# A decoder layer: the GRU's 128-row products as pairs of 64-row products

## What is computed

```python
Pn = rmsnorm(P, input_norm_w)                # P: (4, 64, 256)
k_proj, v_proj = Pn @ Wk.T, Pn @ Wv.T
for _ in range(3):                           # slots: (4, 1024, 256)
    q_proj = rmsnorm(slots, slot_norm_w) @ Wq.T
    scores = einsum('bkd,bmd->bkm', q_proj, k_proj) * SCALE
    attn = softmax(scores, axis=-2)          # over the 1024 slots
    attn = attn / (sum(attn, axis=-1, keepdims=True) + EPS)
    updates = einsum('bkm,bmd->bkd', attn, v_proj)
    slots = gru_cell(updates, slots, ...)    # r, z, n gates
```

## Time and profile before

| | us |
|---|---|
| median of three runs | 556.05 (555.78 to 556.29) |
| the profiled execution | 555.52 |
| its span, first to last instruction | 553.7 |
| PE busy | 504.1 |
| weight loads (PEld) busy | 363.6 |
| VectorE busy | 440.0 |
| ScalarE busy | 340.5 |
| GpSimd busy | 251.7 |
| products of line L1456, 1,128 of them | 149 to 484 of the span |

### The profile page before, as it was taken

How to read it: one execution, slowest core, us unless ns; L and a number is a source line. 1 busy time by engine, 2 the same in 40 slices (tenths; PEclk the granted TensorE clock), 3 DMA queues, 4 the chain that set the end, 5 groups by cost and what they waited for, 6 DMA issues and landing times.

```text
span 553.7 us, 7262 instructions
## 1 busy us (share of the span) xinstructions
PE 504.1 (91%) x2154; PEld 363.6 (66%) x2154; DVE 440.0 (79%) x794; ACT 340.5 (61%) x600; POOL 251.7 (45%) x217
## 2 busy tenths in 40 slices
PE   6999986959779999899999999999997999979992
PEld 2465552725557687488768867885885788767771
DVE  2999999998799487989967985897677567868882
ACT  4557539784697574667466656765663766557452
POOL 0123050400223256556835664575335156737776
PEclk9999999879889999999999999999997999989997
DMA  8950435420021031000000000002111136255742
GB/s 286 336 189 2 124 67 140 125 78 1 0 77 72 6 78 77 0 2 0 2 0 1 0 0 1 1 2 76 40 38 38 39 126 237 87 163 161 235 138 71
DMA packets 30661, 43.13 MB, mean 78 GB/s; under 512 B 7933, under 2 KB 22398, under 8 KB 30336
## 3 DMA queue, kind: packets, MB, share of 16 engines
q1 hardware_dynamic: 27216, 34.25, 20.5%
q0 software_dynamic: 3408, 8.43, 4.2%
HBM read 25.70 MB, written 16.83 MB: 77 GB/s over the span
## 4 chain that ended last, share of the span: by engine, by line
PE 51%; issue 6%; DVE 6%; POOL 4%; ACT 3%; DMA 1%; SPq 0%; POOLq 0%; ACTq 0%; DVEq 0%
PE psum L1456 35%; PE psum L1549 7%; PE psum L1267 3%; PE psum L1398 2%; PE psum L1520 2%; PE psum L1344 1%; POOL gru L1019 1%; DVE gru L1872 1%; POOL out L1057 1%; POOL sorted_rows L1049 1%; DVE slots_full L1874 1%; POOL slots_lo L1034 1%; PE psum L1356 1%; DVE gru L1852 1%; PE psum L1420 1%
## 5 line engine op out<-in xcount | busy, mean ns | idle before, releaser
L1456 PE MATMUL psum<-slots_hi,w_hh 128*128 128x512 f32 x560 | 181.5, 406 | 1.2 <-ACT gru L766 1.2
L1456 PEld LDWEIGHTS psum<-slots_hi,w_hh 128*128 128x128 f32 x560 | 104.5, 191 | 27.9 <-issue 4.2
L1019 POOL TENSOR_TENSOR gru<-slots_full,gru 128x512 f32<-128x512 f32 x43 | 65.9, 1531 | 111.6 <-ACT gru L772 111.6
L1456 PE MATMUL psum<-slots_lo,w_hh 128*128 128x512 f32 x280 | 112.3, 401 | 0.0
L1456 PE MATMUL psum<-at,v_ih_pair 128*128 128x512 f32 x288 | 92.6, 406 | 4.6 <-DVE at L1751 3.1
L772 ACT ACTIVATE gru<-gru,vec 128x512 f32<-128x512 f32 x48 | 34.7, 722 | 59.1 <-DVE gru L1852 59.0
L1456 PEld LDWEIGHTS psum<-at,v_ih_pair 128*128 128x128 f32 x288 | 54.6, 193 | 21.6 <-DVE at L1751 3.4
L1845 DVE SCALAR_TENSOR_TENSOR gru<-psum,vec,gru 128x512 f32<-128x512 f32 x48 | 35.9, 748 | 35.6 <-PE psum L1456 29.8
L1152 PE MATMUL psum<-early_hi,w_in 128*128 128x512 f32 x128 | 57.3, 606 | 5.2 <-DMA early_hi<-in_xT 5.1
L1456 PEld LDWEIGHTS psum<-slots_lo,w_hh 128*128 128x128 f32 x280 | 53.4, 191 | 12.9
L1872 DVE TENSOR_TENSOR gru<-gru 128x512 f32<-128x512 f32 x47 | 43.7, 930 | 7.2 <-POOL gru L1019 3.7
(11 more groups left out here) (249 smaller groups left out, 868.1 us busy)
## 6 DMA issues: line engine op xcount, KB each, us to landing
gathered<-sorted_rows SPq DMA_DIRECT2D x39, 129.0 KB, 2.4
x_scratch<-slots_full SPq DMA_DIRECT2D x8, 512.0 KB, 3.0
x_block<-x_scratch SPq DMA_DIRECT2D x8, 512.0 KB, 4.3
early_hi<-in_xT SPq DMA_DIRECT2D x3, 1024.0 KB, 5.7
v_ih_pair<-value_part SPq DMA_DIRECT2D x32, 96.0 KB, 2.2
x_tm<-in_x SPq DMA_DIRECT2D x4, 512.0 KB, 7.0
slots_full<-expert_plus SPq DMA_DIRECT2D x1, 2048.0 KB, 10.1
sorted_rows<-gru SPq DMA_DIRECT2D x1, 1032.0 KB, 11.4
```

Source lines behind the costliest of these rows:

```text
L1019: pool.tensor_tensor(DF(u), full[:, c, seq(k, h), blk(j)], X(u), ALU.subtract).then_inc(d_pool, 1)
L1456: last = pe.matmul(psum[:, bank, :], w, d, start=start and i == 0, stop=stop and i == len(pairs) - 1, skip_group_check=begun or late)
```

## The change

From unit (1,1) to unit (4,6), 30 units, every product on 128 rows becomes two products on 64 rows each, one with the lower half of the partitions ("low rows") and one with the upper ("high rows"). `both` writes them in turns. The two of a pair go to different banks, as they belong to different sums: the low rows run ahead and the high rows follow. In a unit the low rows do r, hn, xn and z of their own unit; the high rows do xn and z of the unit before and then r and hn. The high rows of a sum begin only when its low rows are done, by the new semaphore `low_rows`, on which PE waits for itself.

Of the four half products in a gate's update, low weight by low attention is left out. The product with the low weight is needed on one half only, and is given to the low or the high rows so that both have the same number: 45 half products a unit. For this the high attention must also be had on the other half, in `at_x`, to which SP copies it by a DMA of 64 rows for each h (`copy_attention`).

`attention` and its spread for h = 0 are made in two halves of 512 tokens, the first between t2 of unit 6 and mix of unit 5, the second after it. The spread for h = 1 goes ahead of candidate of unit 2, `tops` behind candidate of unit 3. Mean squares stay in unit 2, but stand after its first eight or nine pairs, scores stand there in unit 3 and sums in unit 6 (before: in unit 5, after xn). ScalarE's and GpSimd's orders are as before; the counts they wait for are adapted.

```diff
+        def at_made(k, h, j):
+
+            n = 2 * k + h
+            return n + 1 + n // 2 - (1 if k > 0 and h == 0 and j == 0 else 0)
...
+        at_x = parts_of_value[:, 0:T]
...
+                def copy_attention(k, h):
+
+                    n = 2 * k + h
+                    sp.wait_ge(at_hi, at_made(k, h, J - 1))
+                    if n > 2:
+                        sp.wait_ge(at_copied, 16 * (n - 2))
+                    if k > 1:
+                        sp.wait_ge(z_mm, U * (n - 1))
+                    sp.dma_start(at_x[half(1 - h), :].bitcast(F32),
+                                 at[n % 3][half(h), :].bitcast(F32)).then_inc(at_copied, 16)
+
+                copy_attention(1, 0)
                 sp.dma_start(ew_dram, expertT).then_inc(plus_out, 16)
...
+                def both(lows, highs):
+
+                    low = high = None
+                    for i in range(max(len(lows), len(highs))):
+                        if i < len(lows):
+                            bank, w, d, start = lows[i]
+                            low = pe.matmul(psum[:, bank, :], w, d, start=start, stop=False, skip_group_check=True)
+                        if i < len(highs):
+                            bank, w, d, start = highs[i]
+                            high = pe.matmul(psum[:, bank, :], w, d, start=start, stop=True, skip_group_check=True)
+                    return low, high
...
+                def split_unit(k, q, before, between=None, last=False):
...
+                    def hidden(bank, gate, rows):
+                        return [(bank, wh[w][rows, i, cols(gate)], slots[d][rows, i, b, blk(j)],
+                                 rows == lo and (i, w, d) == (0, 0, 0)) for i in range(C) for w, d in PASSES]
+
+                    def update(bank, gate, rows, with_low):
+                        first = [(bank, vp(0, b)[rows, cols(gate)], a[rows, blk(j)], rows == lo and gate == 2)]
+                        high_part = a if rows == half(h) else at_x
+                        return first + [(bank, vp(1, b)[rows, cols(gate)], high_part[rows, blk(j)], False)][0:with_low]
+
+                    r_hid, hn_lo = hidden(r, 0, lo), hidden(hn, 2, lo)
+                    r_hi, hn_hi = hidden(r, 0, hi) + update(r, 0, hi, 0), hidden(hn, 2, hi)
...
+                        pe.wait_ge(t_dve, u - 1)
+                        one, two = r_hid, hn_lo
...
+                    if x_before:
+                        pe.wait_ge(low_rows, 4 * n_split - 5)
+                    low, high = both(one[0:2], x_before)
+                    if x_before:
+                        high.then_inc(xn_mm, 1)
+                        pe.wait_ge(low_rows, 4 * n_split - 4)
+                    low, high = both(one[2:], z_before[0:4])
...
+                    if q % J == 0 and q // J < J + 1:
+                        pe.wait_ge(at_lo, at_made(k, h, j))
...
+                    if not swapped:
+                        low, high = both(update(r, 0, lo, 1), z_before[4:6])
+                        low.then_inc(low_rows, 1)
+                        pe.wait_ge(r_act, u)
+                        low, high = both(two[0:max(nz - 6, 1)], z_before[6:])
+                        two = two[max(nz - 6, 1):]
+                        if z_before:
+                            high.then_inc(z_mm, 1)
+                    if "R" in between:
+                        between["R"]()
...
+                        pe.wait_ge(low_rows, 4 * n_split - 3)
+                        n = len(two)
+                        low, high = both(two, r_hi[0:n])
+                        low.then_inc(low_rows, 1)
+                        highs = r_hi[n:]
...
+                    if last:
+                        low, high = both([], highs)
+                        high.then_inc(r_mm, 1)
+                        pe.wait_ge(low_rows, 4 * n_split - 2)
+                        low, high = both([], hn_hi)
+                        high.then_inc(hn_mm, 1)
+                        pe.wait_ge(t2_dve, u)
+                        for w in range(2):
...
+                        mm.then_inc(z_mm, 1)
+                        return [], []
+                    pe.wait_ge(t2_dve, u)
+                    low, high = both(update(XN_B, 2, lo, 0), highs[0:1])
+                    low.then_inc(low_rows, 1)
+                    highs = highs[1:]
...
+                    pe.wait_ge(z_act, u - 1)
+                    z_lo = hidden(z, 1, lo) + update(z, 1, lo, u % 2)
+                    n = len(highs)
+                    low, high = both(z_lo[0:n], highs)
...
+                        high.then_inc(r_mm, 1)
+                        pe.wait_ge(low_rows, 4 * n_split - 2)
+                        low, high = both(z_lo[n:], hn_hi)
+                        high.then_inc(hn_mm, 1)
+                    low.then_inc(low_rows, 1)
+                    return update(XN_B, 2, hi, 1), hidden(z, 1, hi) + update(z, 1, hi, 1 - u % 2)
...
+                rest = [], []
                 for k in range(1, LAST):
-                    unit(k, 0)
-                    unit(k, 1)
-                    unit(k, 2, {"HN": lambda: mean_squares(k + 1)})
-                    scores(k + 1)
-                    unit(k, 3)
-                    unit(k, 4)
-                    unit(k, 5, {"XN": lambda: sums(k + 1)})
-                    unit(k, 6)
+                    if k == 1:
+                        unit(k, 0)
+                    else:
+                        rest = split_unit(k, 0, rest)
+                    rest = split_unit(k, 1, rest)
+                    rest = split_unit(k, 2, rest, {"R": lambda: mean_squares(k + 1)})
+                    rest = split_unit(k, 3, rest, {"R": lambda: scores(k + 1)})
+                    rest = split_unit(k, 4, rest)
+                    rest = split_unit(k, 5, rest)
+                    rest = split_unit(k, 6, rest, {"R": lambda: sums(k + 1)}, last=k + 2 == PAIRS)
                     if k + 2 < PAIRS:
-                        unit(k, 7)
+                        rest = split_unit(k, 7, rest)
...
+                def attention(f, j):
                     dve.wait_ge(d_rd, f + 1)
-                    dve.scalar_tensor_tensor(out=sc[:], in0=sc[:], scalar=small[:, 3:4], in1=inv[:],
-                                             op0=ALU.mult, op1=ALU.mult).then_inc(attn_done, 1)
-                    dve.wait_ge(attn_done, f + 1)
-
-                def spread_attention(f, h):
+                    dve.scalar_tensor_tensor(out=sc[:, blk(j)], in0=sc[:, blk(j)], scalar=small[:, 3:4],
+                                             in1=inv[:, blk(j)], op0=ALU.mult,
+                                             op1=ALU.mult).then_inc(attn_done, 1)
+                    dve.wait_ge(attn_done, J * f + j)
+
+                def spread_attention(f, h, cols, made):
...
+                def first_of_pair(f, j):
+                    attention(f, j)
+                    spread_attention(f, 0, blk(j), at_made(f, 0, j))
+
+                def second_of_pair(f):
+                    spread_attention(f, 1, slice(0, T), at_made(f, 1, 0))
...
                     settle(k, 0)
                     if k == 1:
                         lows(B - 1, H2 // 2, H2)
+                    second_of_pair(k)
                     candidate(k, 2)
-                    spread_attention(k, 1)
                     settle(k, 1)
+                    candidate(k, 3)
                     tops(k + 1)
-                    candidate(k, 3)
                     settle(k, 2)
                     candidate(k, 4)
...
                     candidate(k, 6)
+                    first_of_pair(k + 1, 0)
                     settle(k, 5)
-                    attention(k + 1)
+                    first_of_pair(k + 1, 1)
                     if not later:
                         gate_centre()
-                    spread_attention(k + 1, 0)
                     candidate(k, 7)
                     if not later:
-                        spread_attention(LAST, 1)
+                        second_of_pair(LAST)
                         score(0)
                     settle(k, 6)
```

108 lines of the change are left out of this document (87 added, 21 removed).

## The result

The changed kernel takes 566.68 us (median of four executions, 565.94 to 567.51), the kernel before, run beside it, 555.91 us (555.11 to 556.29). The ratio is 1.0195, 95% interval 1.0177 to 1.0214. The forecast was 561.2 us, with 558 to 564.5 as its own range: slower is right, but the measured time lies outside that range, and the loss is twice what I had worked out. The profiled execution took 567.29 us, its span is 565.5.

The account below looks back on a forecast made before the run. TensorE's queue was taken as the bound, busy 51.5 of 51.6 us a pass. Passes +4.2, start -1.2 and end +2.2 make +5.2 on the profiled 555.52, so 560.7; the runs' median lies 0.5 above: 561.2 us, range 558 to 564.5.

Parts of the forecast that it names:

- A pair is one slot, and its loads are covered: TensorE: two 64-row products take the time of one whole product, 0.2325 us, their weight loads hidden beneath products.
- a dearer pair: Rival, TensorE: a pair takes 0.25 us because both halves write 128-column outputs at once; 567 us, chance 0.07.
- the two extremes: Rivals, TensorE: a load shown with each pair (632 us) or no overlap of pairs (706 us); chance 0.03 together.
- the clock: Rival: granted clock falls at each second stop of a pass, costing 1.5 to 3.1 us a pass; 566 to 570, chance 0.10.
- two signs of being wrong: Wrong if VectorE's work around the attention takes 1.4 us less than laid out, or pairs cost other than a slot.
- Two stops a pass: TensorE waits for r(5) in unit 6, 1.15 us, and for t2(7) in the next pass's unit 0, 2.45 us.
- +1.4 us a pass: Passes from U4 of k = 1 to U4 of k = 4: each 53.0 us for 51.6, +4.2 for three.
- U4: The start of a pass's unit 4 on TensorE, 289.36 us in k = 2, from which the forecast counts.
- The start, "-1.2": Pass k = 1: unit (1,2) meets mean squares at the same 222.1, U4 comes at 236.6 for 237.76, 1.2 us sooner.
- The end, "+2.2": Pass k = 4: r(6) comes 1.6 us later, the order with s(5) in the middle adds some 0.6; +2.2 us.
- PE keeps the lead: Rival, same two waits: stops a pass are short, measurably faster from 1.5 us down, 550.4 without any; chance 0.26.

Follow-up runs that it names:

- all_three: Changed kernel with squares(k, 1) behind r_gate(k, 5), squares(k, 2) behind r_gate(k, 7), settle(k, 5) ahead of the first token half: 557.47 us.
- squares1: Changed kernel with squares(k, 1) behind r_gate(k, 5) on ScalarE instead of ahead of it: 562.63 us.
- settle_first: Changed kernel with settle(k, 5) ahead of first_of_pair(k + 1, 0) on VectorE, so both token halves stand together: 561.98 us.
- start_only: Changed kernel with candidate(0, 7) between the first token halves in the first pass and attention copies issued per token half: 564.85 us.
- squares2: Changed kernel with squares(k, 2) behind r_gate(k, 7) on ScalarE: 571.99 us.
- copy_halves: all_three with the second token half behind candidate(k, 7), except in pass 4, and attention copies issued per token half: 561.52 us.
- pairs_alone: settle_first with sums back in unit 5, second_of_pair behind candidate(k, 2) and tops ahead of candidate(k, 3): 565.09 us.
- sums_back: Changed kernel with sums(k + 1) back in unit 5 instead of unit 6: 576.53 us.
- half_last: copy_halves with difference(k, 7) ahead of add_squares(k, 2) on GpSimd and the second token half behind settle(k, 7), passes 1 to 3: 568.85 us.

## Why the forecast was right in kind and half in size

**A pair is one slot, and its loads are covered.** Right: 0.233 us; all_three's remainder gives 49.5 us for a pass against 49.4 forecast. The rivals "a dearer pair" and the two extremes are refuted. The measured 566.7 us is near what two rivals give, 567 for the dearer pair and 566 to 570 for the clock, but neither is what happened: the pair cost its slot, and the clock stayed up at the second stops. Neither of my two signs of being wrong came either: VectorE's work around the attention took more than laid out, not less.

**Two stops a pass.** Right in place and releaser: squares1 takes the first away, and settle_first more than halves the second. Mis-sized is the term "+1.4 us a pass": it measured +2.13, 2.2 us over the three. The first stop is 0.2 to 0.3 larger, since the chain from r(4) to the end of r(5) took 9.73 us and not 9.45. The second, 3.0 for 2.45, since t2(7) ended 29.9 us after U4 (r(4) less the forecast's 3.92) and not 29.05, of which TensorE's own lateness takes back 0.2: r(6) came 0.3 late, a half 1.95 us from start to start and not 1.8 (twice), and the s(5) beside GpSimd took 1.67 us, 1.0 over its length alone and not 0.8.

**The start, "-1.2".** This step failed. I let unit (1,2) meet the mean squares at 222.1 with no new stop before them; they began at 224.00, after stops of 1.66 and 1.35 us, and the clock fell behind these. U4 of pass 1 came 0.8 us later than before, not 1.2 sooner (239.9 against 237.76 and the 1.3 us of scatter): 2.0 us. I had kept VectorE's durations in the first pass as they were and not asked whether r(1,1), behind squares(0,3) and s(0,7), would still be ahead of TensorE. It wasn't ahead even before: TensorE stood 1.22 us for it at 220.24. So shorter work of TensorE ahead of it could gain nothing there, and the new order made r(1,1) later by 0.6 us (221.43 for 219.52 and the scatter). start_only shows it: with VectorE's candidate(0, 7) one half sooner the first stop shrinks from 1.66 to 0.26 us, the second stays as it was (1.38), the clock stays up, and the start is 3.15 us shorter.

**The end, "+2.2".** Measured +3.75 from U4 (r(5,0) 37.55 us after it against 33.8). r(4,6) came 0.35 later than laid out, and from it to r(5,0) 21.46 us against 19.63 before, +1.8 for my 0.6. With settle_first's order 1.1 us of it are gone, so the order with s(5) in the middle costs about twice what I gave it; in the changed kernel TensorE stands there for gate_centre, 2.63 us. The other 0.8 us of the last stage's loss stay with settle_first's order, and no experiment takes them apart. The sum of the three terms is off by 2.2 + 2.0 + 1.55, less 0.2 behind r(5,0): the 5.5 us between 561.2 and 566.7.

**The clock.** I had put it at the second stop, with 0.10. It stayed at 1.00 there. It fell at the start, where it hadn't before, and in pass 4 (0.50 from 430 to 432), where it had in the kernel before too. squares2 and copy_halves show how near the passes were, and pairs_alone that the length of a stop doesn't decide it alone. That the changed kernel's passes were spared may be partly luck.

**"PE keeps the lead" (0.26)** needed stops under 1.5 us a pass. They were 4.4; even all_three has 1.7 and ends within 0.3% of before.

**Open.** That no order can reach 49.5 us isn't shown; five were tried. In sums_back the part of the loss outside the profiled execution is unexplained.

## What to carry to other kernels

TensorE was busy 51.5 of 51.6 us, but by the forecast's own working r(5) came only 2.4 us, and t2(7) only 1.6 us, before TensorE needed them. The 2 us by which the bound engine was shortened all became stops, and another 2 with them, as the paired results come later and the new order delays t2(7). Before making the busiest engine faster, lay out what the next chain needs, in every stage (the first and the last pass too), with the later arrival of its inputs: interleaving two sums brings the early result of each at the end of both. And a mend is read by where the stop goes: here one unbroken stop of 2.63 us cost 1.5 us a pass more than two short ones of nearly the same sum.

## What the runs showed of the hardware

- Pairs of 64 x 128 fp32r products, low and high rows in two banks, start within 0.02 us of each other (a few up to 0.04), and pairs 0.233 us apart, as the 128-row products did at 0.2325; a load of 64 rows (0.18 us) runs beneath products of its own rows.
- A stop of 1.71 and one of 0.74 us with six pairs between left the granted clock at 1.00 (changed kernel); one of 2.63 (squares2) or 3.40 us (half_last) was followed by a mean of 0.63 over 3.2 us and 0.57 over 4.0, parts at 1.00 and parts at 0.50, the lower level. At the start, idle of 1.66 and 1.35 us with one pair between was followed by 0.50 for 3.4 us (changed kernel), and idle of 0.26 and 1.38 with one pair between left it at 1.00 (start_only). The length of a stop doesn't decide alone: in pairs_alone the same stop for the stack was followed by 0.55 over 2 us in one pass (1.65 us, at 250.63) and by 1.00 in the next (1.66, at 304.82). Nor is the moment fixed: in squares2 products ran 0.8 us at 1.00 behind the stop at 326.73, while behind the one at 270.26 they ran at 0.50 from the first.
- VectorE's instruction from SBUF to SBUF on 128x512 takes 0.69 or 0.74 us alone and up to 1.67 or 1.68 beside one of GpSimd's, in the rows above; those that read PSUM (t, t2) took 0.75 and 0.69 in either case. So the cost of a VectorE order depends on which of its instructions meets GpSimd's: in settle_first 0.9 us moved from s(5) to the second half.
